# Where the rotary sums of an attention unit are formed: from accumulating DMAs to GpSimd and TensorE

## The reference, cut to what matters

```
q = gelu(x @ Wq) + 0.21;   k = gelu(x @ Wk) + 0.21;   v = x @ Wv
rope(t) = t * cos + xr(t) * sin        # xr swaps the two channels of each pair: (-t1, t0)
z   = 1 / (q . mean(k) + 1e-6)
kv  = rope(k)^T v / n                  # 16 x 16 for each head
out = (rope(q) @ kv) * z
h   = layernorm(out + x)
```

## Time and profile before

| what | value |
|---|---|
| median of 3 runs | 1821.69 us (1821.29 to 1822.49) |
| profiled execution | 1821.29 us, its span 1819.5 us |
| PE busy over the span | 1784.0 us (98%) |
| DVE, ACT, POOL busy | 1454.6, 927.9, 945.0 us |
| PE clock granted, mean | 0.994 |
| one attention unit (from one `sum_k` to the next, at 426 us) | 24.87 us |
| DMA of `kr<-kc`, `qc<-qs`, to landing | 7.0 and 6.7 us |

### The profile page before, as it was taken

One profiled execution on the slowest core, in us unless ns is written; L12 is line 12 of the kernel. 1 busy time (PEld: TensorE's weight loads), 2 busy tenths in 40 slices (PEclk: granted clock), 3 DMA queues, 4 the chain that ended last, 5 costly groups with the idle time before them and its releaser, 6 DMA issues.

```text
span 1819.5 us, 41765 instructions
## 1 busy us (share of the span) xinstructions
PE 1784.0 (98%) x17084; PEld 1438.9 (79%) x17084; DVE 1454.6 (80%) x3422; ACT 927.9 (51%) x1741; POOL 945.0 (52%) x743
## 2 busy tenths in 40 slices
PE   9999999999999999999998999999999999999998
PEld 3336788888888888888886988888888888888887
DVE  3667888888888888888886858787888888888887
ACT  4554666777667777667775733333333323322221
POOL 1556798888898888988882012121212121222221
PEclk9999999999999999999998999999999999999999
DMA  7374564454547653544548911010101010101000
GB/s 291 149 265 144 151 164 94 81 119 83 117 94 198 166 126 74 126 94 101 122 106 250 301 66 47 24 47 24 44 27 36 34 36 35 35 32 39 24 12 24
DMA packets 34800, 182.14 MB, mean 100 GB/s; under 512 B 6000, under 2 KB 6832, under 8 KB 21296
## 3 DMA queue, kind: packets, MB, share of 16 engines
q0 software_dynamic: 10880, 79.70, 20.4%
q1 hardware_dynamic: 20960, 89.62, 13.8%
q10 hardware_dynamic: 2768, 10.15, 1.4%
HBM read 80.89 MB, written 31.46 MB: 62 GB/s over the span
## 4 chain that ended last, share of the span: by engine, by line
PE 53%; POOL 35%; issue 6%; DVE 3%; DMA 2%; ACT 1%; ACTq 0%; SPq 0%; POOLq 0%; DVEq 0%
PE bankC L1431 13%; POOL yB L789 8%; POOL yB L792 8%; POOL qs L800 7%; PE bankC L32 7%; PE bankC L33 7%; PE bankC L34 7%; PE bankC L1430 6%; POOL qc L799 5%; PE conv_ps L256 3%; PE hid_ps L245 3%; POOL rstdB L815 3%; POOL qc L807 3%; POOL kr L773 1%; PE turn L1405 1%
## 5 line engine op out<-in xcount | busy, mean ns | idle before, releaser
L1431 PE MATMUL bankC<-down,act_hi 128*128 128x512 f32 x992 | 353.1, 397 | 0.0
L1430 PE MATMUL bankC<-down,act_lo 128*128 128x256 f32 x868 | 246.2, 284 | 0.0
L1431 PEld LDWEIGHTS bankC<-down,act_hi 128*128 128x128 f32 x992 | 186.3, 188 | 41.9
L1556 DVE TENSOR_TENSOR act_lo<-gel,act_hi 128x512 fp32r<-128x512 f32 x256 | 210.6, 823 | 8.7
L32 PE MATMUL bankC<-aT_hi,up_hi 128*128 128x512 f32 x512 | 199.6, 390 | 0.0
L33 PE MATMUL bankC<-aT_lo,up_hi 128*128 128x512 f32 x512 | 199.6, 390 | 0.0
L34 PE MATMUL bankC<-aT_hi,up_lo 128*128 128x512 f32 x512 | 199.4, 389 | 0.0
L1510 POOL TENSOR_TENSOR hC<-hC,vecC 128x1024 f32<-128x1024 f32 x16 | 38.8, 2426 | 284.0 <-PE turn L1405 284.0
L1516 POOL TENSOR_TENSOR rstdC<-var_epsC,minus_halfC 128x4 f32<-128x4 f32 x47 | 56.1, 1193 | 248.6 <-DVE var_epsC L1584 248.6
L1430 PEld LDWEIGHTS bankC<-down,act_lo 128*128 128x128 f32 x868 | 164.0, 189 | 1.4
L1473 ACT ACTIVATE aT_hi<-turn 128x512 fp32r<-128x512 f32 x64 | 34.8, 596 | 234.8 <-PE turn L1405 234.8
(11 more groups left out here) (211 smaller groups left out, 5173.3 us busy)
## 6 DMA issues: line engine op xcount, KB each, us to landing
kr<-kc POOLq DMA_DIRECT2D x32, 1024.0 KB, 7.0
qc<-qs POOLq DMA_DIRECT2D x64, 512.0 KB, 6.7
raw_late<-in_AB SPq DMA_DIRECT2D x30, 320.0 KB, 3.7
u<-hA SPq DMA_DIRECT2D x8, 1024.0 KB, 5.0
u_next<-u SPq DMA_DIRECT2D x8, 1024.0 KB, 5.2
hC<-u SPq DMA_DIRECT2D x16, 512.0 KB, 4.1
xC<-in_x SPq DMA_DIRECT2D x16, 512.0 KB, 4.9
out<-w_flat SPq DMA_DIRECT2D x15, 512.0 KB, 2.6
```

Source lines behind the costliest of these rows:

```text
L1430: e.matmul(bank[:, 0:H], a_lo[:, fb, tok], both[k][:, fb, 0, :], start=False, stop=False)
L1431: m = e.matmul(bank[:, :], a_hi[:, fb, tok], both[k][:, fb, :, :].rearrange("p a h -> p (a h)"), start=fb == 0, stop=fb == FB - 1)
L1556: e.tensor_tensor(a_lo[:, fb, :], g, a_hi[:, fb, :].bitcast(F32), ALU.subtract).then_inc(s_act_lo, 1)
```

## The change

The accumulating DMAs go. The sum for k is done by POOL: four `tensor_tensor` additions of 128 x 512, one for each pair of token tiles. The sum for q is not formed at all. Since the swap of channels can be moved from q to the other factor, `kv_rot = rot @ kv` is formed by one matmul with a constant 128 x 128 matrix (`turn_kv`), copied from PSUM to SBUF by DVE (`copy_turned`), and `outputs` accumulates `kv * qc + kv_rot * qs` in PSUM: 64 matmuls where there were 32. The table `sin_q` loses its alternating sign, and `rot` is loaded beside the masks.

The order changes too. `outputs(n-1)` moves between `turn_k` 1 and 2, and `turn_kv(n-1)` stands ahead of `turn_k` 0. On POOL `invert(n-2)` moves from the end of the unit to directly behind `residual`.

The diff, cut to the code that works:

```diff
-            def sum_k(n):
-                w.wait_ge(s_ks, 4 * n + 4)
-                e.dma_start(flat(kr), flat(kc), accum_op=ALU.add).then_inc(d_kr, 16)
+            def sum_k(n, u):
+                w.wait_ge(s_ks, 4 * n + u + 1)
+                e.tensor_tensor(kr[:, u, :], kr[:, u, :], kc[:, u, :], ALU.add).then_inc(s_kr, 1)
...
-            def sum_q(n):
-
-                w.wait_ge(s_qr, 3 * n + 3)
-                w.wait_ge(s_qd, n + 1)
-                for a in range(2):
-                    e.dma_start(flat(qc)[a::2, :], flat(qs)[1 - a::2, :], accum_op=ALU.add).then_inc(d_qr, 16)
...
+            def turn_kv(n):
+                w.wait_ge(d_consts, 3 * 16)
+                w.wait_ge(s_kvw, n + 1)
...
+                e.matmul(big[0][:, 0:CB * D], rot[:, :], kv[:, :, :].rearrange("p c n -> p (c n)"),
+                         start=True, stop=True).then_inc(s_rot, 1)
+
             def outputs(n):
-                w.wait_ge(d_qr, 2 * 16 * (n + 1))
-                w.wait_ge(s_kvw, n + 1)
+                w.wait_ge(s_qr, 3 * n + 3)
+                w.wait_ge(s_qd, n + 1)
+                w.wait_ge(s_kvr, n + 1)
...
+                    for wt, q in ((kv, qc), (kv_rot, qs)):
+                        for j in range(QUARTERS):
+                            for i in range(GR):
...
+                                m = e.matmul(out, wt[ch, db, :], quarter(q[ch, db, :], j), start=q is qc, stop=q is qs)
...
+                if n >= 1:
+                    turn_kv(n - 1)
                 turn_k(n, 0)
                 turn_k(n, 1)
+                if n >= 1:
+                    outputs(n - 1)
                 turn_k(n, 2)
                 turn_k(n, 3)
-                if n >= 1:
-                    outputs(n - 1)
...
+            def copy_turned(n):
+                w.wait_ge(s_rot, n + 1)
+                w.wait_ge(s_out, n)
+                e.tensor_copy(kv_rot[:, :, :].rearrange("p c n -> p (c n)"),
+                              big[0][:, 0:CB * D]).then_inc(s_kvr, 1)
```

More of the change, by code:

```diff
@@ L639, in attention_phase @@
         y_rows = [place[f"yB{s}"] for s in range(LANES)]
-        kr, qc, qs, gT, v, gain, shift, kv_mask, mean_mask = (
-            place[n] for n in ("kr", "qc", "qs", "gT", "v", "gain", "shift", "kv_mask", "mean_mask"))
+        kr, qc, qs, gT, v, gain, shift, rot, kv_mask, mean_mask = (
+            place[n] for n in ("kr", "qc", "qs", "gT", "v", "gain", "shift", "rot", "kv_mask", "mean_mask"))
         w_all = [keep["w_first"], keep["w_second"]]
@@ L653, in attention_phase @@
         kv = sb("kv", [P, CB, D])
+        kv_rot = sb("kv_rot", [P, CB, D])
         gelu_shift = sb("gelu_shift", [P, 1])
@@ L672, in attention_phase @@
         s_memset, s_hT, s_hi, s_lo, s_mul, s_res = (sem(n) for n in ("memset", "hT", "hi", "lo", "mul", "res"))
-        s_k, s_gk, s_kt, s_ks, d_kr, d_qr = (sem(n) for n in ("k", "gk", "kt", "ks", "d_kr", "d_qr"))
+        s_k, s_gk, s_kt, s_ks, s_kr = (sem(n) for n in ("k", "gk", "kt", "ks", "kr"))
         s_q, s_gelu, s_gq, s_qr, s_qd, s_v, s_vs = (sem(n) for n in ("q", "gelu", "gq", "qr", "qd", "v", "vs"))
         s_ksum, s_km, s_den, s_dens, s_dent, s_z = (sem(n) for n in ("ksum", "km", "den", "dens", "dent", "z"))
-        s_kv, s_kvm, s_kvw = (sem(n) for n in ("kv", "kvm", "kvw"))
+        s_kv, s_kvm, s_kvw, s_rot, s_kvr = (sem(n) for n in ("kv", "kvm", "kvw", "rot", "kvr"))
         s_out, s_turned, s_scaled, s_y = (sem(n) for n in ("out", "turned", "scaled", "y"))
@@ L822, in gpsimd @@
                 residual(n)
-                if n < 2:
+                if n >= 2:
+                    invert(n - 2)
+                else:
                     for g in (2 * n, 2 * n + 1):
                         conv.last.gpsimd(e, w, g)
-                sum_k(n)
+                for u in range(DUOS):
+                    sum_k(n, u)
                 for x, db in ((0, 0), (0, 1), (1, 0)):
                     rotate_q(n, x, db)
-                sum_q(n)
-                if n >= 2:
-                    invert(n - 2)
             then(e, lambda g: invert(UNITS - 2 + g))
@@ L922, in outputs @@
                 for db in range(CB):
[L923 to L927, removed]
+                    for wt, q in ((kv, qc), (kv_rot, qs)):
+                        for j in range(QUARTERS):
+                            for i in range(GR):
+                                ch = slice(D * i, D * i + D)
+                                out = big[i][D * j:D * j + D, :].rearrange("p (a d c) -> p a d c", a=TILES, d=CB)[:, :, db, :]
+                                m = e.matmul(out, wt[ch, db, :], quarter(q[ch, db, :], j), start=q is qc, stop=q is qs)
                 m.then_inc(s_out, 1)
@@ L953, in tensor @@
             key_value(UNITS - 1)
+            turn_kv(UNITS - 1)
             outputs(UNITS - 1)
@@ L1164, in vector @@
                     measure(n - 2, 1)
+                if n >= 1:
+                    copy_turned(n - 1)
                 if n == 0:
@@ L1184, in vector @@
             key_value(UNITS - 1)
+            copy_turned(UNITS - 1)
             def last(k):
@@ L1742, in gpsimd @@
             last(0)
-            wait_free(Waits(e), before.free["masks"])
+            wait_free(Waits(e), before.free["ring"])
             e.memset(zero[:, :].bitcast(F32), 0.0).then_inc(s_zero, 1)
@@ L1889, in build @@
         under(ctx, [("w_first", weights, F32R)], [("w_flat", [P, 4 * 3 * H])])
-        under(ctx, [("kv_mask", [P, CB, 32]), ("mean_mask", [P, CB, 32])], [("zero", [P, 512], F32R)])
+        under(ctx, [("rot", [P, P]), ("kv_mask", [P, CB, 32]), ("mean_mask", [P, CB, 32])], [("zero", [P, 512], F32R)])
         under(ctx, [("raw_late", [P, 3, width])], [("act1_hi", [P, 8, 512], F32R)], [("cos_k", rows), ("sin_k", rows)])
@@ L1927, in load_tables @@
             e.dma_start(flat(place["shift"]), t["shift_rows"].partition_broadcast(P)).then_inc(keep["d_rows"], 16)
+            e.dma_start(place["rot"][:, :], t["rot"]).then_inc(keep["d_masks"], 16)
             e.dma_start(flat(place["kv_mask"]), t["kv_mask"]).then_inc(keep["d_masks"], 16)
@@ L2033, in layout @@
     d["cos_k"], d["sin_k"] = rows(cos), rows(sin * sign)
-    d["cos_q"], d["sin_q"] = cols(cos), cols(-sin * sign)
+    d["cos_q"], d["sin_q"] = cols(cos), cols(sin)
+    i = np.arange(0, 128, 2)
+    rot = np.zeros((128, 128), np.float32)
+    rot[i + 1, i], rot[i, i + 1] = 1, -1
+    d["rot"] = rot
     p = np.arange(128)
```

16 lines of the change are left out of this document (10 added, 6 removed).

## The result

The changed kernel takes 1832.9 us (median of 7 runs, 1831.7 to 1835.8), the kernel before 1823.6 beside it (7 runs): a ratio of 1.0052, 95% interval 1.0040 to 1.0064. It is slower by 9 us; 26 were forecast. The sign and the range held, the size did not. The profiled execution took 1829.6 us, 8.3 more than that of before.

What follows compares the result with a forecast made beforehand. PE, busy 98% of the span, was taken to bound the kernel. +0.91 us a unit over 31 units (+28), +4.3 at the start and -6.5 at the end gave +26 on 1821.7: 1848 us, range 1830 to 1870.

Steps and rivals of the forecast that it cites:

- Two more rounds, +1.35: PE's outputs, each unit: two further rounds of small matmuls cost 1.35 us, bounds 0.78 and 1.43.
- rival 1: PE's outputs: rounds pack tightly, two more cost 0.9 us, the unit grows by 0.46 us, total 1834 us; chance 0.14.
- turn_kv, +0.25: PE, each unit: the added float32 matmul of 64 columns costs 0.25 us, bounds 0.1 and 0.5.
- Stalls that go, -0.69: PE, each unit: waits for the last gelu of k (0.23), kr 3 (0.36) and DVE's third sum (0.1 us) vanish.
- Unit, +0.91: One attention unit on PE: rounds and turn_kv less vanished stalls give +0.91 us, bounds +0.18 and +1.6.
- POOL, the copy, the power: Beside PE, each unit: additions of 1.25 us, DVE copy about 0.2 us, moved power and product; all cost nothing.
- rival 3: POOL becomes the bound: additions take 1.9 us or more, unit 26.6 us or more, total 1873 us; chance 0.08.
- rival 4: DVE's copy is shut out by POOL until T + 4.0, outputs start 3 us later each unit, total 1940 us; chance 0.03.
- Rival 2: PE's outputs: two further rounds cost 0.5 us in all, the unit is 0.1 us shorter, total 1814 us; chance 0.07.
- Start of attention, +4.3: First unit: POOL's four additions hold DVE's line 135 some 4 us longer, delaying PE: +4.3 us (0 to 6).
- End of attention, -6.5: Last unit: outputs come 5.3 us earlier without the DMA wait, most half-clock loss returns: -6.5 us (-3.5 to -7.5).
- theory F: For the run without turn_kv: PE waits for its next 16 KB of instructions; gaps would repeat every 7 units, not 6.

Runs made afterwards that it cites:

- The two runs on the order: Outputs moved between turn_k 1 and 2 in the kernel before: ratio 0.9937; outputs put back behind turn_k 3 in the changed kernel: ratio 1.0118.

## Why the prediction was wrong in size, point by point

- **The bound.** Right: PE 99.66 of 100 us, POOL with 1.9 us to spare in a unit.
- **Two more rounds, +1.35.** Measured +1.26 (2.69 - 1.43), 0.63 a round. With it rival 1 falls, though its 1834 us lies nearer to the result: it was near by the errors at the start and the end, not by its reason. An estimate from the Trainium skill ("TensorE: Matmul & The Clock Gate", Part 3), one matmul's 0.39 us and 4 ns for each of 15 further tiles, is 0.45 us a round; the trace does not agree.
- **turn_kv, +0.25.** +0.16 in the timeline, 0.15 by its removal.
- **Stalls that go, -0.69.** The undisturbed unit grew by 0.70, so the stalls gave 1.26 + 0.16 - 0.70 = 0.72 us. The two runs on the order show that most of it comes from the move of the outputs: 0.49 in the kernel before, 0.66 in the changed one. The 0.69 was near.
- **Unit, +0.91.** +0.70 undisturbed; with the long units +0.86. The sum was near its value with a part missing: (8.5 - 3.7) / 30 = 0.16 us are mostly gaps of PE in the four rounds, which no step held.
- **POOL, the copy, the power.** As foreseen: additions 5.05 us for four, so rival 3 falls (at 1.9 us an addition its own terms make a unit of 27.1 us, not 26.6); the copy 0.23 us with no wait of PE on it in the loop, so rival 4 falls; the place of the power worth nothing. Rival 2 needed two rounds under 0.6 us.
- **Start of attention, +4.3: the step that failed.** It measured -7.1, which is 11.4 of the 17.7 us by which the sum missed. The step read one row, 7.72 us up to the end of POOL's row, as "held until POOL is through", and lengthened the row. The runs show that a row of POOL holds line 135 only where it follows a DMA issue; otherwise DVE gets in at the next boundary, after 0.2 to 0.5 us. The change takes the DMA away, and two waits of PE with it: the hold goes, and with it the 2.56 us for hT_lo; the DMA's flight goes, and with it the 1.85 us for kr (at 180.81 in the trace of before), to which the step had given nothing. The trace of before held the contrary case 11 us earlier, beside unit 0's residual (a row of DVE, then one of POOL):

```profile
162.83 0.45 DVE L135 TENSOR_SCALAR minus_meanA<-momentsA 128x4 f32<-128x4 f32 x1
160.85 4.75 POOL L792 TENSOR_TENSOR yB<-yB,shift 128x1024 f32<-128x1024 f32 x2
```

Line 135 was through at 163.28, as the first of these two operations ended (163.26), with the second still to run to 165.60 and no DMA issue ahead of them. The Trainium skill ("SBUF — State Buffer", Who interferes with whom) says that of a DVE instruction in a two-port mode and a GpSimd instruction the one that issues first has the shared ports "for the whole instruction", and that a DMA does not contend with a compute engine. The rows of 0.48, 0.45, 0.27 and (DMA alone) 0.18 us agree; the 7.72 us over six instructions is more than that rule gives.
- **End of attention, -6.5.** -5.6 up to the composition as forecast (-5.3), then -4.8 more where 1.2 were expected. Of these 2.2 us lie ahead of the last gelu of the feed-forward blocks (the saved half clock is part of them), and 2.5 us behind the last stores' issue: 5.8 us to the end of the span before, 3.3 after. For this last piece the sum had no term. It is POOL's closing DRAIN, before and after:

```profile
L1972 POOLq DRAIN  x1: 6533/6533/6533, 1812.7 to 1812.7; - x1
L1992 POOLq DRAIN  x1: 1429/1429/1429, 1823.6 to 1823.6; - x1
```

Before, it takes 6.53 us and ends 0.2 us ahead of the end of the span, 2.9 us after SyncE has seen the last store land. After, it takes 1.43 us and is over 2.8 us ahead of the end, so that the last store ends the program.

Adding up: 4.3 + 27 - 6.5 = 25 (the forecast counted 31 units, 26), measured -7.1 + 25.8 - 10.4 = +8.3.

## What to carry to other kernels

A single long duration beside another engine's row has at least two readings; look for the same operation beside the same row in another place, and ask what differs, before lengthening it. A change with several parts is worth taking apart: here one part (the order) was worth -11 us and was hidden under the cost of another (two more rounds), and the costly form paid in the first and the last unit, where nothing hides a DMA. A gain at a start is kept only if every later wait moves with it. And where DMAs are taken away, the end of the program belongs in the sum too.

## What the runs showed of the hardware that was not expected

**PE seems to run out of instructions.** The weight loads of PE in a long unit of the changed kernel:

```profile
600.38 0.65 PEld L934 LDWEIGHTS big<-qs,kv_rot 32*32 32x32 f32 x21
602.12 0.16 PEld L934 LDWEIGHTS big<-qs,kv_rot 32*32 32x32 f32 x10 [1.09 <-issue]
```

and the DMA queues from 599.5 to 600.8 us, when nothing else was moving:

```profile
q8 instruction: 1, 0.02, 5.8%
```

This packet, of 16 KB, starts at 599.52 and takes 1.22 us; the gap ends 1.4 us behind it. So it is with all eight gaps: each ends 1.2 to 1.6 us after such a packet has landed. Between gaps six units apart lie 19 packets and 4827 recorded loads and matmuls, nearly 256 for each. In the changed kernel gaps come only where the packet starts 0.50 to 0.71 us behind the start of the four rounds (of nine such starts one, at 0.64, had none); the rounds use 256 instructions in 2.7 us. The one such wait of over half a us in the loop of the kernel before (0.57 us at 887.50) ends 1.45 us behind a packet too. Without turn_kv the packets at the outputs repeat every 7 units, as theory F said, but they fall at 0.4 us and less or 0.9 and more, and with late outputs all but one do (0.56): neither kernel has such a gap in the loop. Forty instructions more moved all gaps by a unit, though there the starts with a gap reach 0.87 us and those at 0.66 and 0.71 had none, so that the start alone does not decide. With accumulating DMAs beside it the same wait can be long: 3.90 us in the run with early outputs, 1.4 us behind a packet as well. That these packets hold PE's next instructions, and that PE waits for them, is inferred from the times, the counts and the move; what decides when a packet is asked for was not tried.

**POOL's row behind its own DMA issue keeps line 135 of DVE out** for 1.25 us per operation (2.81 us for two, 7.72 for six), where without the issue it is 0.2 to 0.5 us beside rows of up to ten. No other instruction of DVE was tried in its place.

**POOL's closing DRAIN is longer the more DMAs POOL has issued.** It takes 1.43 us in the seven kernels with 8 issues by POOL (1152 packets on its queue), 4.04 us with the DMA for k back (40 issues, 5760 packets), and 6.25 to 6.54 us in the eight with 99 to 104 issues (10416 to 10880 packets): about 0.5 us for each 1000 packets. In those eight it ends the program; with 40 issues it is over just as the last store lands. No run was made to tell packets from issues.
